# Softmax sums of a self attention: ScalarE copy and GpSimd power in place of VectorE's reciprocal, for three groups of four

## The chip, the cores and the metric

The kernel runs on one core of a Trainium2 chip. The metric is the device time of one execution in microseconds (us). The engines are TensorE (PE; PEld is its weight load), VectorE (DVE), ScalarE (ACT), GpSimd (POOL) and SyncE (SP). Each runs its own list of instructions strictly in order, and they meet only through counting semaphores.

## What is computed

A block of six residual layers over x (256 tokens of 512 features), of which the first self attention is the one that the change touches. Its reference, cut to what matters (16 heads of 32 features; `act_quant` rounds a tensor to e4m3 with one scale):

```python
qkv = jnp.einsum('bsh,hf->bsf', x, W_qkv)
q8, q_scale = act_quant(q)
k8, k_scale = act_quant(k)
scores = jnp.einsum('bhqd,bhkd->bhqk', q8, k8) * (q_scale * k_scale) / jnp.sqrt(hd)
attn = jax.nn.softmax(scores, axis=-1)
v8, v_scale = act_quant(v)
out = jnp.einsum('bhqk,bhkd->bhqd', attn, v8) * v_scale
return jnp.einsum('bsh,ho->bso', out, W_out) + b_out
```

The layers around it are a cross attention over 4096 context tokens (most of the run), a feed-forward, an attention over the context as memory, a second self attention and a mixture of experts.

## The kernel before

Everything stays on the core, and each engine's list is written out by hand: `tensor_attention`, `vector_attention`, `scalar_attention` and two GpSimd functions are called with k = 0 for the first self attention and k = 1 for the second. The 16 heads are done in four groups f = 0 to 3 of four heads (SHG = 4), 32 partitions to a head, so that one group fills 128 partitions.

For each group the scores are made once to find each query's maximum (`scores`, L1197; VectorE's `maxima`, L1436). `split_maxima` (L1444 to L1450) turns the maxima into three bf16 parts, TensorE turns these (`turn_maxima`, L1207), ScalarE copies them (`move_maxima`, L1363), and `scores_turned` (L1220, L1224) makes the scores the other way round with the maxima subtracted. ScalarE raises them, one 128x512 Exp for each head (`raise_head`, L1373, four for each group). `weigh_group(f)` then makes, on TensorE, the sums of the exponentials (L1242, into `sum_bank(f)`, counted by `as_summed`) and the weighted values (L1250, into `value_bank(f)`, counted by `as_weighed`).

`normalise(f)` on VectorE closes a group: a reciprocal of the 128x256 sums out of PSUM into the tile `inv` (L1458), and one product of value bank, scale and `inv` into the tile xT (L1461), which counts `ao_moved`. `project_out` (L1257) multiplies xT by the output weights on TensorE; each call is two matmul rows of the trace. After it VectorE adds the result to x (L1512), and the next layer norm begins, whose `rstd` GpSimd makes as a power with exponent -0.5 (L130, 128x1).

The order that matters here, on VectorE: `maxima(2)`, `split_maxima(2)`, `normalise(0)`, `maxima(3)`, `split_maxima(3)`, `normalise(1)`, two additions of the output bias (L1504), `normalise(2)`, `normalise(3)`. On TensorE, with f counting up: `scores_turned(f)`, some dummy matmuls on `ident` that keep the engine busy (`stay_awake`, L135), the scores of the next group's last head, `weigh_group(f - 1)`; then `turn_maxima` of the next group. For f = 2 the dummies stand behind a wait for `ao_moved` 1:

```python
elif f == 2 and k == 0:
    e.wait_ge(ao_moved, 1)
    stay_awake(e, W_BANK, 3)
```

`weigh_group(2)` waits for `ao_moved` 2 ahead of its values, because the value bank of groups 0 to 2 is one and the same. The last stretch is `project_out(1, 0)`, `weigh_group(3)`, and `project_out` of the feature blocks 1, 2, 3 for tokens 0 to 127 and then for tokens 128 to 255. GpSimd has no part in the four groups: `gpsimd_quantise` (L1521) makes three maxima over all partitions before them, and `gpsimd_norm` comes after them.

Of the kernel before, what the change touches and what calls it, by code (L numbers as in the profile page):

```python
# [6 lines left out]
F32 = mybir.dt.float32  # L7
# [3 lines left out]
ALU = mybir.AluOpType  # L11
# [3 lines left out]
P = 128  # L15
T, D = 256, 512
TT, DT = T // P, D // P
# [46 lines left out]
def build(nc, a, out):  # L64
    ctx = ExitStack()
    with ctx:
        def sems(names):
            return [ctx.enter_context(nc.semaphore(n)) for n in names.split()]
# [6 lines left out]
        def place(offset, *specs):  # L75
            places[0] += 1
            with ExitStack() as scope:
                if offset:
                    sb(f"gap{places[0]}", [P, offset // 4], F32, scope)
                return [sb(n, shape, dt, scope) for n, shape, dt in specs]  # L80
# [19 lines left out]
        own = Steps(vector_step)  # L100
# [43 lines left out]
        def norm_move(e, n, i, bank):  # L144
            e.wait_ge(ln_turned, TT * n + i + 1)
            e.copy(xT[:, :, i * P:(i + 1) * P], bank.rearrange("p (c t) -> p c t", c=4)).then_inc(ln_xT, 1)
# [935 lines left out]
        SHG = P // SHD  # L1082
        RING = 2 * SHG

        def att_memory(tag):
            return place(
                WORK, (f"{tag}w_qkv", [P, 3, DT, D], F32), (f"{tag}w_out", [P, DT, D], F32), (f"{tag}b_out", [P, D], F32),
                (f"{tag}b_qk", [P, 8], F32), (f"{tag}b_v", [P, D], F32), (f"{tag}xn", [P, TT, D], F32),
                (f"{tag}qkT", [P, 8, T], F32), (f"{tag}v", [P, TT, D], F32), (f"{tag}q8", [P, 4, T], BF16), (f"{tag}k8", [P, 4, T], BF16),
                (f"{tag}v8", [P, TT, D], F32), (f"{tag}eT", [P, RING, TT * T], F32), (f"{tag}inv", [P, T], F32),  # L1090
                (f"{tag}mx", [P, 2, TT, SHG], F32), (f"{tag}rest", [P, TT, SHG], F32), (f"{tag}sc", [P, 32], F32))

        att_mem = (att_memory("l0_"), att_memory("l1_"))
        w_gate, w_router = place(WORK + 82 * KB, ("w_gate", [P, DT, NE0], F32), ("w_router", [P, DT, E], F32))

# [8 lines left out]
            "mag_found mag_max quant_scaled quant_mag quant_val quant_done")  # L1104
        as_done, as_max, as_negs, as_turned, as_moved, as_doneT, as_raised, as_summed, as_weighed, ao_moved = sems(
            "as_done as_max as_negs as_turned as_moved as_doneT as_raised as_summed as_weighed ao_moved")
        att_out, att_added = sems("att_out att_added")

        W_BANK = twin[:, D:2 * D]

# [4 lines left out]
        def turned_bank(r):  # L1115
            return banks[3 + r][:] if r < 3 else twin[:, 0:D]

        def sum_bank(f):

            return W_BANK[:, T:2 * T] if f < 2 else banks[(0, 5)[f - 2]][:, 0:T]  # L1120

        def value_bank(f):
            return W_BANK[:, 0:T] if f < 3 else banks[4][:, 0:T]

        def qk_bank(k, n):

            return banks[n][:] if k == 0 or n in (0, 2) else (banks[3][:], twin[:, 0:D])[n // 2]

        def v_bank(k, i):
            return banks[4 + i][:] if k == 0 or i == 0 else W_BANK  # L1130
# [51 lines left out]
                e.dma_start(b_v[:], a["l1_bv"].partition_broadcast(P)).then_inc(att_b_in, 16)  # L1182

        def tensor_attention(e, k):
            w, w_out, _, _, _, xn, qkT, v, q8, k8, v8, eT, _, _, _, _ = att_mem[k]
            qs, ks, vs = (q8, k8, v8) if k == 0 else (qkT[:, 0:4, :], qkT[:, 4:8, :], v)
            base = SH * k

# [142 lines left out]
        def att_mags(k):  # L1331

            xn, eT = att_mem[k][5], att_mem[k][11]
            return eT[:, RING - 2:RING, :].rearrange("p a b -> p (a b)"), xn[:].rearrange("p i d -> p (i d)")

        def scalar_attention(e, k):
            _, _, _, b_qk, _, _, qkT, v, _, _, _, eT, _, _, _, sc = att_mem[k]
            tensors = (qkT[:, 0:4, :], qkT[:, 4:8, :], v[:])

            def scale_to_e4m3(n):  # L1340
                t = tensors[n]
                m = att_mags(k)[n % 2].rearrange("p (a b) -> p a b", a=t.shape[1])
                e.wait_ge(quant_scaled, n + 1)
                if n == 2:
                    e.wait_ge(quant_done, 1)
                e.activation(m, t, ACT.Copy, scale=sc[:, 22 + n:23 + n]).then_inc(quant_mag, 1)
                e.wait_ge(quant_mag, n + 1)
                e.activation(t, t, ACT.Copy, scale=sc[:, 6 + n:7 + n]).then_inc(quant_val, 1)

            def move_qk(f):  # L1350
                e.wait_ge(qk_projected, 4 * k + QK_ORDER[k].index(f) + 1)
                if k == 0:
                    t = e.copy(qkT[:, f - 1:f + 1, :].rearrange("p a t -> p (a t)"), qk_bank(k, f // 2))
                else:
                    for g in (f - 1, f):
                        t = e.activation(qkT[:, g, :], qk_bank(k, f // 2)[:, (g % 2) * T:(g % 2 + 1) * T], ACT.Identity, bias=b_qk[:, g:g + 1])
                t.then_inc(qk_moved, 1)

            def move_maxima(f):
                e.wait_ge(as_turned, 4 * k + f + 1)  # L1360
                if f >= 2:
                    e.wait_ge(as_doneT, 4 * k + f - 1)
                e.copy(negsT[:, f % 2, :], turned_bank(0)[:, 0:T]).then_inc(as_moved, 1)  # L1363

            def raise_head(f, r):
                h = SHG * f + r
                if r == 0:
                    e.wait_ge(as_doneT, 4 * k + f + 1)
                    if f >= 2:
                        e.wait_ge(as_weighed, 4 * k + f - 1)  # L1370
                if k == 0 and h == RING - 2:
                    e.wait_ge(quant_done, 3)
                e.activation(eT[:, h % RING, :], turned_bank(r), ACT.Exp,  # L1373
                             scale=sc[:, 9:10] if k == 0 else A_SCALE).then_inc(as_raised, 1)

            if k == 0:
                for i in range(TT):
                    norm_move(e, 1, i, banks[2 * i][:])
            else:
                norm_move(e, 4, 1, av_bank(1))  # L1380
                e.wait_ge(att_b_in, ATT_B[1])
            for f in QK_ORDER[k][0:2]:
                move_qk(f)
            if k == 0:
                scale_to_e4m3(0)
            for f in QK_ORDER[k][2:4]:
                move_qk(f)
            if k == 0:
                scale_to_e4m3(1)
                for i in range(TT):  # L1390
                    e.wait_ge(av_projected, i + 1)
                    e.copy(v[:, i, :], v_bank(k, i)).then_inc(av_moved, 1)
                scale_to_e4m3(2)
            for f in range(4):
                move_maxima(f)
                for r in range(SHG):
                    raise_head(f, r)

        def vector_attention(e, k):
            _, _, b_out, _, b_v, xn, qkT, v, q8, k8, v8, _, inv, mx, rest, sc = att_mem[k]  # L1400
            tensors = (qkT[:, 0:4, :], qkT[:, 4:8, :], v[:])

            def largest(n):
# [46 lines left out]
                e.tensor_tensor(parts[:, :, :, 2], rest[:], parts[:, :, :, 1], ALU.subtract).then_inc(as_negs, 1)  # L1450

            def normalise(f):
                e.wait_ge(as_summed, 4 * k + f + 1)
                if f < 2:
                    e.wait_ge(as_weighed, 4 * k + f + 1)
                if f:
                    e.wait_ge(ao_moved, 4 * k + f)
                own.done(e.reciprocal(inv[:], sum_bank(f)))  # L1458
                own.wait(e)
                e.wait_ge(as_weighed, 4 * k + f + 1)  # L1460
                e.scalar_tensor_tensor(xT[:, f, :], value_bank(f), sc[:, 5:6] if k == 0 else 1.0, inv[:],  # L1461
                                       ALU.mult, ALU.mult).then_inc(ao_moved, 1)
# [27 lines left out]
            for f in range(1, 4):  # L1490
# [7 lines left out]
                if f == 1 and k:  # L1498
                    add_v_bias(1)
            normalise(1)  # L1500
            if k == 0:
                e.wait_ge(att_b_in, ATT_B[0])
# [12 lines left out]
                norm_apply(e, n_norm, i, xn_next)  # L1515

        def gpsimd_quantise(e):
            sc = att_mem[0][-1]
            for n in range(3):
                e.wait_ge(mag_found, n + 1)  # L1520
                e.partition_all_reduce(sc[:, n:n + 1], sc[:, 10 + n:11 + n], P, bass.bass_isa.ReduceOp.max).then_inc(mag_max, 1)  # L1521

        w_up, w_down, w_exp, _, hT, xn3, g3 = place(
            WORK, ("w_up", [P, DT, D], F32), ("w_down", [P, DT, D], F32), ("w_exp", [P, DT, D], F32),
            ("gap_wout", [P, DT * D + 2 * D + 8], F32),
            ("hT", [P, DT, T], F32), ("xn3", [P, TT, D], F32), ("g3", [P, 64], F32))
# [156 lines left out]
        def av_bank(i):  # L1685
            return twin[:, i * D:(i + 1) * D]
# [787 lines left out]
```

## Time and profile before

| | |
|---|---|
| median of 3 runs | 1639.95 us (1639.75 to 1640.92) |
| the profiled execution | 1641.43 us, its span from first to last instruction 1639.6 us |
| mean granted TensorE clock | 0.999 |
| busy share of the span | PE 98%, VectorE 66%, ScalarE 42%, GpSimd 8% |
| the first self attention's four groups | from about 1191.6 to 1223.6 us of the span |

A row of a timeline gives the start in us from the span's start, how long it lasts, the engine, the line of the kernel, the operation with what it writes and reads, how many instructions were merged, and in brackets the idle time ahead of it with the engine that ended it. A row of merged instructions lasts from the first one's start to the last one's end. A row of the chain of waits gives start, length and what the run's end was waiting for at that time, "issue" being time in which the engine waited for nothing that the profile shows. Matmul ends are modelled, and durations on GpSimd are rough.

### The profile page before, as it was taken

What the parts mean: (1) busy time and instruction counts of PE and PEld (TensorE: products, weight loads), DVE (VectorE), ACT (ScalarE), POOL (GpSimd) and SP (SyncE); (2) the same over time, 40 slices, a digit from 0 to 9 for tenths busy, and PEclk for the clock granted to TensorE, in tenths of its full rate; (3) what the DMA queues carried; (4) which work ended last, traced back from release to release, by engine and by line L of the source; (5) the groups of instructions that cost most, each with busy time, mean ns of one, the idle gap of its engine ahead of it and who ended that gap; (6) DMA issues with size and microseconds to landing.
All of it is one profiled execution on the core that took longest, in us unless ns stands there. A gap on an engine that the chain in (4) does not pass through costs nothing.

```text
span 1639.6 us, 22511 instructions
## 1 busy us (share of the span) xinstructions
PE 1611.7 (98%) x8732; PEld 1250.7 (76%) x8732; DVE 1086.7 (66%) x1733; ACT 690.1 (42%) x933; POOL 131.0 (8%) x218
## 2 busy tenths in 40 slices
PE   9999999999999999999999999999999999999998
PEld 7887888888888888888888888887757746555454
DVE  4445777777778778777777779999583741743333
ACT  4334454444445454444454446555331321322221
POOL 0001000000100000010000001111100000011110
PEclk9999999999999999999999999999999999999999
DMA  7876655554565556555454454334320517479994
GB/s 237 226 227 189 161 132 154 149 151 122 170 163 142 148 142 154 119 184 142 119 138 124 128 135 123 102 92 150 121 112 18 205 52 287 197 233 427 422 423 183
DMA packets 125513, 282.93 MB, mean 173 GB/s; under 512 B 7712, under 2 KB 83680, under 8 KB 119264
## 3 DMA queue, kind: packets, MB, share of 16 engines
q1 hardware_dynamic: 103104, 200.75, 38.8%
q0 software_dynamic: 22304, 80.75, 16.5%
q8 instruction: 70, 1.15, 0.3%
q14 instruction: 35, 0.29, 0.1%
HBM read 206.99 MB, written 74.48 MB: 172 GB/s over the span
## 4 chain that ended last, share of the span: by engine, by line
PE 84%; DVE 8%; issue 3%; ACT 3%; DMA 2%; POOL 0%; SPq 0%; DVEq 0%; ACTq 0%
PE bank L478 19%; PE bank L41 19%; PE bank L448 17%; PE bank L500 6%; PE bank L2109 5%; PE bank L1728 3%; PE bank L499 3%; PE bank L2148 2%; PE bank L2134 2%; PE bank L526 1%; DVE e_parts L851 1%; PE bank L2138 1%; DVE S L830 1%; PE bank L2094 1%; DMA v_dram<-v_out 1%
## 5 line engine op out<-in xcount | busy, mean ns | idle before, releaser
L478 PE MATMUL bank<-wv_parts,cT_hi 128*128 128x512 f32 x1024 | 333.8, 390 | 1.7 <-DMA wv_parts<-wv_dram 1.6
L478 PEld LDWEIGHTS bank<-wv_parts,cT_hi 128*128 128x128 f32 x1024 | 192.3, 188 | 42.4 <-DMA wv_parts<-wv_dram 2.0
L851 DVE TENSOR_TENSOR e_parts<-S,e_parts 128x1024 fp32r<-128x1024 f32 (+1 forms) x129 | 156.8, 1215 | 85.5 <-ACT e_parts L656 83.3
L448 PE MATMUL bank<-cT_hi,wk_hi 128*128 128x512 f32 x512 | 204.7, 400 | 0.7 <-DVE cT_lo L783 0.7
L448 PE MATMUL bank<-cT_hi,wk_lo 128*128 128x512 f32 x512 | 199.8, 390 | 0.0
L448 PE MATMUL bank<-cT_lo,wk_hi 128*128 128x512 f32 x512 | 199.7, 390 | 0.0
L647 ACT ACTIVATE S<-S 128x1024 f32<-128x1024 f32 (+1 forms) x129 | 135.8, 1053 | 151.7 <-DVE S L830 151.1
L478 PE MATMUL bank<-wv_parts,cT_lo 128*128 128x512 f32 x512 | 199.3, 389 | 0.0
L843 DVE TENSOR_TENSOR esum<-esum,S 128x512 f32<-128x512 f32 x210 | 144.9, 690 | 71.7 <-ACT S L647 68.1
L656 ACT CAST e_parts<-S 128x1024 fp32r<-128x1024 f32 (+1 forms) x129 | 134.8, 1045 | 135.7 <-PE bank L500 129.5
L803 DVE TENSOR_TENSOR mx<-mx,S 128x512 f32<-128x512 f32 x222 | 152.8, 688 | 13.5 <-ACT S L641 9.6
L830 DVE TENSOR_TENSOR S<-S,mrow 128x1024 f32<-128x1024 f32 (+1 forms) x129 | 155.4, 1207 | 0.4 <-POOL mrow L1050 0.4
L500 PE MATMUL bank<-e_parts,v_back 128*128 128x512 f32 x424 | 154.2, 397 | 0.0
L41 PE MATMUL bank<-q_hi,k_hi 128*128 128x256 f32 x512 | 146.1, 285 | 4.6 <-DVE k_lo L790 4.5
L41 PE MATMUL bank<-q_lo,k_hi 128*128 128x256 f32 x512 | 144.8, 283 | 0.0
L41 PE MATMUL bank<-q_hi,k_lo 128*128 128x256 f32 x512 | 144.8, 283 | 0.0
L625 ACT CAST k_hi<-bank 128x512 fp32r<-128x512 f32 x128 | 75.3, 588 | 156.6 <-PE bank L448 156.6
L641 ACT COPY S<-bank 128x1024 f32<-128x1024 f32 x128 | 129.1, 1009 | 13.5 <-PE bank L41 8.3
L1037 POOL DMA_DIRECT2D v_back<-v_dram x110 | 59.1, 537 | 837.4 <-PE bank L500 826.9
L499 PE MATMUL bank<-e_parts,v_back 128*128 128x256 f32 x424 | 122.9, 290 | 0.2
L856 DVE TENSOR_TENSOR v_out<-bank,v_out 128x512 fp32r<-128x512 f32 x112 | 76.9, 686 | 62.9 <-ACT v_out L668 62.9
L448 PEld LDWEIGHTS bank<-cT_hi,wk_lo 128*128 128x128 f32 x512 | 96.2, 188 | 22.5 <-issue 2.2
(289 smaller groups left out, 2588.4 us busy)
## 6 DMA issues: line engine op xcount, KB each, us to landing
w<-in_w_moe SPq DMA_DIRECT2D x32, 2304.0 KB, 16.6
v_dram<-v_out SPq DMA_DIRECT2D x112, 512.0 KB, 5.0
v_back<-v_dram POOLq DMA_DIRECT2D x110, 512.0 KB
ctx_nat<-in_ctx SPq DMA_DIRECT2D x8, 1024.0 KB, 4.9
ctx_raw<-in_ctxT SPq DMA_DIRECT2D x7, 1024.0 KB, 8.5
v_dram<-v_back SPq DMA_DIRECT2D x14, 512.0 KB, 4.5
v_late<-v_dram POOLq DMA_DIRECT2D x14, 512.0 KB
wv_parts<-wv_dram POOLq DMA_DIRECT2D x6, 1024.0 KB, 8.7
```

Source lines behind the costliest of these rows:

```text
L41: last = e.matmul(dst, lhs, rhs, start=(n == 0), stop=(n == len(terms) - 1))
L448: t = e.matmul(banks[b][:], l, r, start=(c == 0 and m == 0), stop=(c == DT - 1 and m == 2))
L478: t = e.matmul(banks[b][:], l, r, start=(c == 0 and m == 0), stop=(c == DT - 1 and m == 2))
L499: e.matmul(*low, start=False, stop=False)
L500: t = e.matmul(*wide, start=False, stop=(j == NCH - 1 and i == CT - 1))
L641: e.copy(S[:, j * CT:(j + 1) * CT, :].rearrange("p a t -> p (a t)"), twin[:]).then_inc(s_stored, 1)
L647: e.activation(Sj, Sj, ACT.Exp).then_inc(raised, 1)
L656: e.copy(e_place(n)[:, 0, of_chunk(0, m), :], S[:, of_chunk(j, m), :]).then_inc(e_rounded, 1)
L803: own.done(e.tensor_tensor(mx[:], mx[:], two, ALU.max))
L830: e.tensor_tensor(Sj, Sj, mrow[:].unsqueeze(1).to_broadcast([P, CT if m is None else CT // 2, T]), ALU.subtract).then_inc(shifted, 1)
L843: e.tensor_tensor(esum[:], esum[:], two, ALU.add).then_inc(e_summed, 1)
L851: e.tensor_tensor(lo, S[:, of_chunk(j, m), :], hi.bitcast(F32), ALU.subtract).then_inc(e_split, 1)
```

## The change

For the first self attention alone (k = 0) and for groups 0, 1 and 2, VectorE's reciprocal is taken out of `normalise`. ScalarE copies the sums out of PSUM into a new tile `sums` in SBUF (`copy_sums(f)`, placed after the Exps of group f + 1), and GpSimd raises them to the power -1 into `inv` with a tensor_tensor whose second operand is a 128x1 tile of -1.0 broadcast over 256 columns. VectorE then only waits for `sums_inverted` and multiplies. Group 3, and all of the second self attention, keep the reciprocal on VectorE.

```diff
+            def copy_sums(f):
+                e.wait_ge(as_summed, f + 1)
+                if f < 2:
+                    e.wait_ge(as_weighed, f + 1)
+                if f:
+                    e.wait_ge(sums_inverted, f + 1)
+                e.copy(sums[:], sum_bank(f)).then_inc(sums_copied, 1)
+
             for f in range(4):
                 move_maxima(f)
                 for r in range(SHG):
                     raise_head(f, r)
+                if f and k == 0:
+                    copy_sums(f - 1)
...
             def normalise(f):
-                e.wait_ge(as_summed, 4 * k + f + 1)
-                if f < 2:
-                    e.wait_ge(as_weighed, 4 * k + f + 1)
-                if f:
-                    e.wait_ge(ao_moved, 4 * k + f)
-                own.done(e.reciprocal(inv[:], sum_bank(f)))
-                own.wait(e)
+                if f < 3 and k == 0:
+                    e.wait_ge(sums_inverted, f + 2)
+                else:
+                    e.wait_ge(as_summed, 4 * k + f + 1)
+                    if f < 2:
+                        e.wait_ge(as_weighed, 4 * k + f + 1)
+                    if f:
+                        e.wait_ge(ao_moved, 4 * k + f)
+                    own.done(e.reciprocal(inv[:], sum_bank(f)))
+                    own.wait(e)
                 e.wait_ge(as_weighed, 4 * k + f + 1)
                 e.scalar_tensor_tensor(xT[:, f, :], value_bank(f), sc[:, 5:6] if k == 0 else 1.0, inv[:],
                                        ALU.mult, ALU.mult).then_inc(ao_moved, 1)
...
         def gpsimd_quantise(e):
...
+            e.memset(minus[:], -1.0).then_inc(sums_inverted, 1)
+            e.wait_ge(sums_inverted, 1)
+            for f in range(3):
+                e.wait_ge(sums_copied, f + 1)
+                if f:
+                    e.wait_ge(ao_moved, f)
+                e.tensor_tensor(inv[:], sums[:], minus[:].to_broadcast([P, T]), ALU.pow).then_inc(sums_inverted, 1)
```

How the lists of instructions stand, at three places. ScalarE, over the four groups (l_eT are the exponentials, negsT the turned maxima; lines with + are new):

```order
 L1363 CAST negsT<-bank 128x256
 L1373 ACTIVATE l_eT<-bank,l_sc 128x512 x4
+L1400 COPY l_sums<-bank 128x256
 L1363 CAST negsT<-bank 128x256
 L1373 ACTIVATE l_eT<-bank,l_sc 128x512 x4
+L1400 COPY l_sums<-bank 128x256
 L1363 CAST negsT<-bank 128x256
 L1373 ACTIVATE l_eT<-bank,l_sc 128x512 x4
+L1400 COPY l_sums<-bank 128x256
```

Each copy of a group's sums stands behind the four Exps of the next group and, but for the last, ahead of the copy of the maxima of the one after. VectorE with the change, from the second group's end on (L1446 are the maxima, L1474 the product into xT, L1471 the reciprocal):

```order
L1446 TENSOR_REDUCE l_mx<-bank 128x2 x4
L1454 TENSOR_SCALAR negs<-l_mx 128x8
L1456 SCALAR_TENSOR_TENSOR l_rest<-l_mx,negs 128x8
L1458 CAST negs<-l_rest 128x8
L1460 TENSOR_TENSOR negs<-l_rest,negs 128x8
L1474 SCALAR_TENSOR_TENSOR xT<-bank,l_sc,l_inv 128x256
L1517 TENSOR_TENSOR x<-x,l_b_out 128x512 x2
L1474 SCALAR_TENSOR_TENSOR xT<-bank,l_sc,l_inv 128x256
L1471 RECIPROCAL l_inv<-bank 128x256
L1474 SCALAR_TENSOR_TENSOR xT<-bank,l_sc,l_inv 128x256
```

Three reciprocals are gone; the products stay where they were, and the fourth group's reciprocal stands behind the third group's product. GpSimd with the change (the rows of ISA without a tile load a library; L1534 are the maxima over partitions):

```order
L1162 CAST ident_bf<-ident 128x128
L1534 ISA
L1534 ISA l_sc<-l_sc 128x1 x3
L1535 MEMSET l_minus 128x1
L1541 ISA
L1541 TENSOR_TENSOR l_inv<-l_sums,l_minus 128x256 x3
L130 TENSOR_TENSOR rstd<-vareps,half 128x1 x4
```

The library load that stood right ahead of the four `rstd` now stands ahead of the three new powers; the `rstd` come behind them.

## Rows read from the trace of the kernel before

**Rows 1.** The page: span, busy time of each engine.

```profile
span 1639.6 us, 22511 instructions
PE 1611.7 (98%) x8732; PEld 1250.7 (76%) x8732; DVE 1086.7 (66%) x1733; ACT 690.1 (42%) x933; POOL 131.0 (8%) x218
```

**Rows 2.** The chain of waits, 1205.9 to 1221.2 us (start, length, what).

```profile
1205.98 1.76 DVE l_inv L1458
...
1211.74 0.27 PE bank L1207 x2
...
1218.26 2.79 PE bank L1257 x6
...
1221.14 0.70 DVE x L1512
```

**Rows 3.** VectorE's timeline, 1205.9 to 1224.3 us.

```profile
1207.77 0.49 DVE L1461 SCALAR_TENSOR_TENSOR xT<-bank,l_sc,l_inv 128x256 f32<-128x256 f32 x1
...
1213.35 0.48 DVE L1461 SCALAR_TENSOR_TENSOR xT<-bank,l_sc,l_inv 128x256 f32<-128x256 f32 x1
...
1217.47 1.76 DVE L1458 RECIPROCAL l_inv<-bank 128x256 f32<-128x256 f32 x1 [0.25 <-PE bank L1242]
1219.26 0.48 DVE L1461 SCALAR_TENSOR_TENSOR xT<-bank,l_sc,l_inv 128x256 f32<-128x256 f32 x1
1221.14 0.69 DVE L1512 TENSOR_TENSOR x<-bank,x 128x512 f32<-128x512 f32 x1 [1.40 <-PE bank L1257]
...
1222.81 0.15 DVE L119 TENSOR_SCALAR vareps<-meanvar 128x1 f32<-128x1 f32 x1
1223.69 0.55 DVE L123 TENSOR_SCALAR xn<-x,meanvar,rstd 128x512 f32<-128x512 f32 x1 [0.73 <-POOL rstd L130]
```

**Rows 4.** TensorE's timeline, 1204.6 to 1223.7 us.

```profile
1204.61 1.05 PE L1250 MATMUL bank<-l_eT,l_v 128*32 128x256 f32 x16
...
1208.31 0.94 PE L135 MATMUL bank<-ident 128*128 128x128 f32 x6 [0.72 <-DVE xT L1461]
...
1210.38 1.05 PE L1250 MATMUL bank<-l_eT,l_v 128*32 128x256 f32 x16
...
1214.30 1.05 PE L1250 MATMUL bank<-l_eT,l_v 128*32 128x256 f32 x16
...
1218.19 5.42 PE L1257 MATMUL bank<-l_w_out,xT 128*128 128x512 f32 x12
```

**Rows 5.** ScalarE's timeline, 1206.5 to 1216 us.

```profile
1206.54 0.37 ACT L1363 CAST negsT<-bank 128x256 bf16<-128x256 f32 x1 [2.50 <-PE bank L1207]
...
1212.05 0.37 ACT L1363 CAST negsT<-bank 128x256 bf16<-128x256 f32 x1 [1.98 <-PE bank L1207]
1213.53 2.42 ACT L1373 ACTIVATE l_eT<-bank,l_sc 128x512 f32<-128x512 f32 x4 [1.11 <-PE bank L1224]
```

**Rows 6.** GpSimd's timeline, 1178 to 1224 us.

```profile
1178.13 0.38 POOL L1521 PARTITION_ALL_REDUCE l_sc<-l_sc  x1 [9.64 <-DVE l_sc L1408]
...
1192.22 0.35 POOL L1521 PARTITION_ALL_REDUCE l_sc<-l_sc  x1 [6.67 <-DVE l_sc L1408]
1223.06 0.60 POOL L130 TENSOR_TENSOR rstd<-vareps,half 128x1 f32<-128x1 f32 x1 [30.48 <-DVE vareps L119]
```

**Rows 7.** One line's operations: L130 (duration in ns: minimum, median, maximum).

```profile
L130 POOL TENSOR_TENSOR rstd<-vareps,half x12: 549/570/1008, 5.7 to 1430.5; 128x1 f32<-128x1 f32 x12
```

**Rows 8.** GpSimd's groups by shape (busy us, mean ns of one).

```profile
L2017 POOL CAST gate_parts<-ids_i 128x128 fp32r<-128x128 int32 x1 | 0.9, 888 | 0.1
...
L1162 POOL CAST ident_bf<-ident 128x128 bf16<-128x128 f32 x1 | 0.3, 287 | 0.0
...
L2014 POOL CAST slot_col<-slot_col_i 128x1 f32<-128x1 int32 x1 | 0.2, 188 | 0.0
```

**Rows 9.** By stretch: PE, PEld, DVE, ACT, POOL busy; granted clock, DMA share, GB/s.

```profile
1206.00:1211.74 5.74, 4.02 (x59) 2.27 (x60) 5.49 (x12) 2.79 (x5) 0.00 (x0) 1.00 0.01 3
```

More of the change, by code:

```diff
@@ L1090, in att_memory @@
                 (f"{tag}v8", [P, TT, D], F32), (f"{tag}eT", [P, RING, TT * T], F32), (f"{tag}inv", [P, T], F32),
-                (f"{tag}mx", [P, 2, TT, SHG], F32), (f"{tag}rest", [P, TT, SHG], F32), (f"{tag}sc", [P, 32], F32))
+                (f"{tag}mx", [P, 2, TT, SHG], F32), (f"{tag}rest", [P, TT, SHG], F32), (f"{tag}sc", [P, 32], F32), (f"{tag}sums", [P, T], F32), (f"{tag}minus", [P, 1], F32))
         att_mem = (att_memory("l0_"), att_memory("l1_"))
@@ L1106, in build @@
             "as_done as_max as_negs as_turned as_moved as_doneT as_raised as_summed as_weighed ao_moved")
-        att_out, att_added = sems("att_out att_added")
+        att_out, att_added, sums_copied, sums_inverted = sems("att_out att_added sums_copied sums_inverted")
         W_BANK = twin[:, D:2 * D]
@@ L1184, in tensor_attention @@
         def tensor_attention(e, k):
-            w, w_out, _, _, _, xn, qkT, v, q8, k8, v8, eT, _, _, _, _ = att_mem[k]
+            w, w_out, _, _, _, xn, qkT, v, q8, k8, v8, eT = att_mem[k][:12]
             qs, ks, vs = (q8, k8, v8) if k == 0 else (qkT[:, 0:4, :], qkT[:, 4:8, :], v)
@@ L1336, in scalar_attention @@
         def scalar_attention(e, k):
-            _, _, _, b_qk, _, _, qkT, v, _, _, _, eT, _, _, _, sc = att_mem[k]
+            _, _, _, b_qk, _, _, qkT, v, _, _, _, eT, _, _, _, sc, sums, _ = att_mem[k]
             tensors = (qkT[:, 0:4, :], qkT[:, 4:8, :], v[:])
@@ L1397, in scalar_attention @@
                     raise_head(f, r)
+                if f and k == 0:
+                    copy_sums(f - 1)
         def vector_attention(e, k):
-            _, _, b_out, _, b_v, xn, qkT, v, q8, k8, v8, _, inv, mx, rest, sc = att_mem[k]
+            _, _, b_out, _, b_v, xn, qkT, v, q8, k8, v8, _, inv, mx, rest, sc, _, _ = att_mem[k]
             tensors = (qkT[:, 0:4, :], qkT[:, 4:8, :], v[:])
@@ L1517, in gpsimd_quantise @@
         def gpsimd_quantise(e):
-            sc = att_mem[0][-1]
+            inv, _, _, sc, sums, minus = att_mem[0][12:]
             for n in range(3):
```

## Prediction

> **What bounds the kernel now.** The page says that TensorE is busy for 98% of the span and VectorE for 66% [rows 1]; such averages say little of a stretch of 20 us, so I read the stretch itself, first in the chain of waits. What the run's end waits for there is VectorE until 1211.6 us, with the first group's reciprocal in the middle of it (1205.98, 1.76 us), and from 1211.74 us TensorE, without a break until VectorE adds the projected tile at 1221.14 [rows 2]. So the first of the reciprocals stands on the path, and the later ones run beside TensorE.
>
> VectorE's timeline gives the moments at which the products into xT start and end: group 0 at 1207.77, group 1 at 1213.35, and group 3 from 1219.26 to 1219.74 [rows 3]. TensorE's timeline tells who waits: its dummy matmuls start at 1208.31, after 0.72 us of idling for group 0's product; the values of group 2, which need group 1's product, start at 1214.30; the last projections start at 1218.19 [rows 4]. The end is tight: the third projection of tokens 0 to 127 needs group 3's product, which ends at 1219.74, and its two predecessors (four of the twelve rows that share 5.42 us) end near 1220.0. A product that comes later is soon paid for one for one.
>
> **The change part by part.** Let X be the time that GpSimd needs for one 128x256 power. Everything else can be read.
>
> *Copies.* Three 128x256 copies out of PSUM by ScalarE, at 0.37 us each, the price of its 128x256 cast out of PSUM [rows 5]. The first comes when the values of group 0 are done, 1204.61 + 1.05 = 1205.66, plus 0.04 from TensorE to ScalarE (1211.74 + 0.27 to 1212.05 [rows 2, 5]): 1205.70 to 1206.07, in the 2.50 us that ScalarE idles ahead of 1206.54. The second can run from 1211.47 to 1211.84, in the idle time ahead of 1212.05. These two cost nothing by themselves. The third stands behind the last four Exps, which end at 1213.53 + 2.42 = 1215.95, so it runs from 1215.99 to 1216.36; nothing of this layer is queued behind it on ScalarE.
>
> *Handovers.* From VectorE to GpSimd it takes 0.10 us (1222.81 + 0.15 to 1223.06), and back 0.03 us (1223.66 to 1223.69) [rows 3, 6]. I use these for ScalarE to GpSimd as well.
>
> *Library load.* The load that stood ahead of `rstd` now stands ahead of the first power, with no wait of its own. The last maximum over partitions ends at 1192.57 and the first copy at 1206.07, 13.5 us later. Ahead of the maxima the same kind of load fitted into an idle time of 9.64 us [rows 6]. I cost it at nothing; were it exposed, it would add what remains of it to group 0. The memset of one column beside it lies in the same gap.
>
> *Group 0.* The power starts at 1206.17, and the product at 1206.20 + X in place of 1207.77: a shift of X - 1.57, which I call D. Behind that wait on VectorE stand the maxima and the split of group 3, and behind these TensorE's turn of the maxima at 1211.74. D goes to the path whole if positive, and also, up to about 0.7 us, if negative.
>
> *Group 1.* The values end at 1210.38 + 1.05 = 1211.43 + D; copy and handovers add 0.04 + 0.37 + 0.10, so the power starts at 1211.94 + D and the product ends at 1212.45 + D + X. TensorE's values of group 2 want that at 1214.30 + D, so up to X = 1.8 nothing waits here.
>
> *Group 2.* This power needs the third copy and, since it overwrites `inv`, group 1's product. The first gives 1216.46 + D, the second 1212.55 + D + X; they cross at X = 3.91. Its product takes 0.03 + 0.48, and only then does VectorE reach group 3's reciprocal (0.04 + 1.76) and product (0.03 + 0.48), where today the reciprocal starts at 1217.47, as soon as its sums are there.
>
> *Sum.* Below the crossing, group 3's product ends at 1216.46 + D + X + 0.51 + 0.04 + 1.76 + 0.51 = 1219.28 + D + X. Against 1219.74 that is D + X - 0.46 = **2X - 2.03**. Above it, it ends at 1212.55 + D + 2X + 2.82 = 1215.37 + D + 2X, which is **3X - 5.94** late. In words: below the crossing one power and the tail are on the path; above it, all three stand in a row. The three reciprocals of 1.76 us that leave VectorE are in these sums already.
>
> *The size of X.* The trace of before has the power only on one column: 549 ns at least, 570 at the median [rows 7]. From below: 0.55 plus 255 columns at the price of a plain cast, (287 - 188) / 127 = 0.78 ns each, is 0.75 us. From above: a one-column cast takes 188 ns, so the arithmetic of the power is 549 - 188 = 361 ns for one column, and if each of 256 columns pays that in turn, X = 0.19 + 92.4 = 92.6 us [rows 7, 8]. Between ends so far apart I take the geometric middle, 8.3 us, moved a little towards the upper end because that one comes from the row of the same operation: **X = 10 us**, which says that the loop overlaps some nine columns. Then D = 8.4 and the sum is 3 x 10 - 5.94 = 24.1 us.
>
> *The clock.* With X = 10 TensorE would idle for more than 8 us at a time. The trace shows nothing like it: even in the stretch around group 0, with TensorE busy 4.02 of 5.74 us, the granted clock is 1.00, the level of 2.4 GHz [rows 9]. A fall to 1.2 GHz would matter only where TensorE sets the pace, in the eight projection rows behind the last wait: 8 x 5.42 / 12 = 3.6 us more at most, none at least. I add the half, 1.8 us. The Trainium skill (TensorE: Matmul & The Clock Gate, section "What's actually happening") says that an idle TensorE falls to half its rate and has to be busy again to regain it; by that it would be the upper end, and no run here shows it yet.
>
> Together 24.1 + 1.8 = 25.9 us. On the profiled execution's own 1641.43 us that is 1667.3; this execution lies 1.48 us above the median of the runs, 1639.95, so for the median I predict **1666 us**.
>
> **The rivals.** *GpSimd is quick enough (no change).* If the columns stream, X lies between the lower end, 0.75, and the price of the slowest plain row, (888 - 188) / 127 = 5.5 ns a column, which gives 0.55 + 1.41 = 1.96 us [rows 8]. The sum is then -0.5 to +1.9 us, with 1.3 us in the middle +0.6: 1640.5 us. It decides for X below 2.65, where 2X - 2.03 reaches 3.3 us. For it: one column costs only 0.36 us more than a cast, which may be depth rather than rate. Against it: streaming at a few ns a column means that a hundred columns are in work at once. The Trainium skill (GPSIMD Engine Reference, section "Elementwise — side-by-side cycle accounting") gives 2.6 cycles an element for an addition with two inputs; an estimate from that page is 256 x 2.6 / 1.2 GHz = 0.55 us on top of the one-column power, X = 1.1 and a change of +0.2 us. It speaks for this rival, but of additions, and no run here shows it. Faster by over 0.2% (3.3 us, about what a measurement of this kernel can tell from no change) cannot come out of the sum: at the lower end of X it is -0.5.
>
> *No overlap at all (much slower).* X = 92.6, the sum 3 x 92.6 - 5.94 = 271.9, with the clock 1913 us. For it: the one-column row taken at its word. Against it: the loop over columns would have to start each only when the one before is finished.
>
> *The powers are not where the wait is.* If the library is loaded only when the first power comes up, its unknown remainder is added to D once. Against it: `rstd` at 1223.06 started 0.10 us after its input, long after its load [rows 6]. I give it no chance of its own.
>
> **How the numbers follow.** Forecast (X from 2.65 to 32): 0.62, with 1643 to 1733 as its own range; X = 32 gives 90.1 + 3.6 us. GpSimd quick: 0.23. Little or no overlap (X over 32): 0.15. The range reaches down to the quick case's lower end, 1639, since without it 0.38 would be left out, and up to 1733; about 0.16 is outside. Slower: 0.62 + 0.15 = 0.77; faster 0.01; the rest, 0.22, within 0.2%.
>
> **What would show it.** In the profile of the changed kernel the three rows of the power give X at once, and the formula then has to give the time: three rows of about 10 us, VectorE idle ahead of each product for the GpSimd tile, TensorE idle ahead of the dummy matmuls by some 9 us and ahead of group 2's values by some 8, the third power starting right after group 1's product. With X near 1 the chain would show TensorE as before, with VectorE's last reciprocal starting near 1218. A time that doesn't fit 2X - 2.03 or 3X - 5.94 for the X that is seen would mean that I have a wait wrong; a granted clock under 1.00 after the idle times would size the last term.

## The result and the profile after

The changed kernel takes 1761.35 us (median of 4 runs, 1760.84 to 1761.66) against 1640.28 us before (4 runs): a ratio of 1.0736, 95% interval 1.0721 to 1.0751. It is slower by 121 us. The prediction said 1666, with a range of 1639 to 1733: the sign was right, the time lies outside the range. The profiled execution has a span of 1759.9 us in place of 1639.6.

The page of the changed kernel, its span, its busy times and one of its costliest groups:

```profile
span 1759.9 us, 22518 instructions
...
PE 1617.5 (92%) x8732; PEld 1252.7 (71%) x8732; DVE 1082.3 (61%) x1730; ACT 690.5 (39%) x936; POOL 254.5 (14%) x222
...
L1541 POOL TENSOR_TENSOR l_inv<-l_sums,l_minus 128x256 f32<-128x256 f32 x3 | 123.7, 41243 | 20.7 <-ACT l_sums L1400 20.0
```

Every engine did about the work that it did before [rows 1]; GpSimd alone has 123.5 us more, and its three powers of 41.2 us take 123.7. Where they lie is told by the chain of waits (start, length, what the end of the run was waiting for):

```profile
1205.99 41.19 POOL l_inv L1541
...
1247.21 0.50 DVE xT L1474
...
1253.45 41.13 POOL l_inv L1541
...
1295.23 41.44 POOL l_inv L1541
...
1337.28 1.77 DVE l_inv L1471
...
1339.61 1.74 PE bank L1257 x2
```

In [rows 2] the same place held one reciprocal of 1.76 us and then TensorE. Now all three powers stand in the chain one behind the other. VectorE's timeline has the places of [rows 3] (start, duration, operation, and in brackets the idle time ahead and what ended it):

```profile
1247.21 0.48 DVE L1474 SCALAR_TENSOR_TENSOR xT<-bank,l_sc,l_inv 128x256 f32<-128x256 f32 x1 [41.44 <-POOL l_inv L1541]
...
1294.60 0.48 DVE L1474 SCALAR_TENSOR_TENSOR xT<-bank,l_sc,l_inv 128x256 f32<-128x256 f32 x1 [42.99 <-POOL l_inv L1541]
...
1336.69 0.48 DVE L1474 SCALAR_TENSOR_TENSOR xT<-bank,l_sc,l_inv 128x256 f32<-128x256 f32 x1 [39.99 <-POOL l_inv L1541]
1337.28 1.76 DVE L1471 RECIPROCAL l_inv<-bank 128x256 f32<-128x256 f32 x1
1339.07 0.48 DVE L1474 SCALAR_TENSOR_TENSOR xT<-bank,l_sc,l_inv 128x256 f32<-128x256 f32 x1
```

VectorE idles 124.4 us for the three tiles. The copies by ScalarE took 0.37 us each, as worked out. TensorE's rows answer to [rows 4]:

```profile
1247.75 1.65 PE L135 MATMUL bank<-ident 128*128 128x128 f32 x6 [40.47 <-DVE xT L1474]
...
1251.57 1.31 PE L1250 MATMUL bank<-l_eT,l_v 128*32 128x256 f32 x16
...
1295.14 1.93 PE L1250 MATMUL bank<-l_eT,l_v 128*32 128x256 f32 x16 [39.58 <-DVE xT L1474]
...
1337.23 2.08 PE L1257 MATMUL bank<-l_w_out,xT 128*128 128x512 f32 x2 [34.82 <-DVE xT L1474]
```

It waits at the places of the prediction's walk, and its first work after a wait is slow: the six dummy rows take 1.65 us in place of 0.94, group 1's values 1.31 in place of 1.05. By stretch (length, busy time of PE, PEld, DVE, ACT and POOL, granted clock, DMA share, GB/s):

```profile
1214.00:1247.00 33.00, 0.00 (x0) 0.00 (x0) 0.00 (x0) 0.00 (x0) 33.00 (x1) 0.50 0.00 0
1247.00:1250.00 3.00, 2.25 (x12) 1.62 (x16) 2.31 (x5) 0.00 (x0) 0.18 (x1) 0.50 0.00 0
1250.00:1254.00 4.00, 4.00 (x40) 1.59 (x42) 1.40 (x5) 0.65 (x2) 0.55 (x1) 0.74 0.00 0
1254.00:1258.00 4.00, 1.57 (x33) 0.69 (x32) 0.00 (x0) 2.42 (x4) 4.00 (x1) 1.00 0.00 0
...
1336.00:1340.00 4.00, 2.46 (x3) 0.89 (x4) 2.73 (x3) 0.00 (x0) 0.66 (x1) 0.50 0.00 0
```

While all engines but GpSimd stand still, the clock granted to TensorE goes to 0.50, the level of 1.2 GHz. TensorE starts again at 1247.75, and the clock is back at 1.00 in the stretch from 1254 us on.

### The profile page after: what moved, and what is told of

The parts are those of the page before. It is cut to its first block, busy times and chain, and to the rows that moved or that the text cites. A ratio compares the mean times of both kernels' runs of the same rounds, so it can differ in the third digit from the quotient of the medians.

```text
span 1759.9 us, 22518 instructions
## 1 busy us (share of the span) xinstructions
PE 1617.5 (92%) x8732; PEld 1252.7 (71%) x8732; DVE 1082.3 (61%) x1730; ACT 690.5 (39%) x936; POOL 254.5 (14%) x222
## 4 chain that ended last, share of the span: by engine, by line
PE 78%; POOL 7%; DVE 7%; ACT 3%; issue 3%; DMA 2%; SPq 0%; DVEq 0%; ACTq 0%; POOLq 0%
PE bank L478 18%; PE bank L41 17%; PE bank L448 16%; POOL l_inv L1541 7%; PE bank L500 6%; PE bank L2129 5%; PE bank L1748 3%; PE bank L499 3%; PE bank L2168 2%; PE bank L2154 2%; PE bank L526 1%; PE bank L2158 1%; DVE e_parts L851 1%; DVE S L830 1%; PE bank L2114 1%
## 5 line engine op out<-in xcount | busy, mean ns | idle before, releaser
L1541 POOL TENSOR_TENSOR l_inv<-l_sums,l_minus 128x256 f32<-128x256 f32 x3 | 123.7, 41243 | 20.7 <-ACT l_sums L1400 20.0
```

The source lines that it names most:

```text
L1541: e.tensor_tensor(inv[:], sums[:], minus[:].to_broadcast([P, T]), ALU.pow).then_inc(sums_inverted, 1)
```

## How the traces are compared

Outside the attention the traces of two executions differ by up to a microsecond or two, so I measure inside the stage: from the start of group 2's maxima on VectorE, the last work that nothing in the change can touch, to the end of group 3's product. The maxima before and in the changed kernel:

```profile
1202.66 2.48 DVE L1436 TENSOR_REDUCE l_mx<-bank 128x2 f32<-128x512 f32 x4
```

```profile
1202.35 2.48 DVE L1446 TENSOR_REDUCE l_mx<-bank 128x2 f32<-128x512 f32 x4
```

Before, that is 1202.66 to 1219.74 [rows 3], 17.08 us. In the changed kernel it is 1202.35 to 1339.55, 137.20 us, so the stage is 120.12 us longer. Of the 120.3 us by which the span grew, that is nearly all.

## The experiments

The theory after the result, A: each column of a power is paid in turn, at 41.2 us / 256 = 0.161 us, and the three powers stand on the path exactly as the prediction's formula has it. Its rivals: a large fixed price or a disturbance by other engines makes 41 us; the time is in the waits around the power; the price hangs on the values.

### e1_probe: the power by itself

In the kernel before, into GpSimd's idle time behind the maxima over partitions:

```diff
+            for n in (1, 2, 4, 8, 16, 32, 64):
+                e.tensor_tensor(tried[:, at:at + n], base[:, 0:n], power[:, 0:1].to_broadcast([P, n]), ALU.pow)
+                at += n
+            e.tensor_tensor(tried[:, at:at + 128], base[:, 0:128], power[:, 0:1].to_broadcast([P, 128]), ALU.mult)
```

and ahead of the second self attention seven powers of 32 columns: a base of 1.5 with the exponents -1, -0.5, 1, 2 and 0, and the bases 100 and 1 with -1.

> The kernel before with powers of 1, 2, 4, 8, 16, 32 and 64 columns and one product of 128 columns added on GpSimd in the idle time behind the three maxima, and seven powers of 32 columns with other exponents and bases in its idle time ahead of the second self attention. Theory A (each column is paid in turn, none overlaps): 41.2 us / 256 = 0.161 us a column, so 64 columns 10.3 to 10.7 us, 32 columns 5.2 to 5.6, and a line through 1 column at 0.55 us; the product of 128 columns under 1 us. Theory B (a large fixed share, such as code fetched at the start, or other engines disturbing GpSimd during the attention): 64 columns far above 10.7 us or the steps not in proportion. If the price hangs on the values (rival to A: a slow path for exponent -1), the seven powers differ by over 10%. The total time stays within 0.2% of before, as all of it lies in idle time.

GpSimd's groups by shape (busy us, mean ns of one, idle time ahead):

```profile
L1538 POOL TENSOR_TENSOR l_tried<-l_base,l_power 128x64 f32<-128x64 f32 x1 | 10.5, 10512 | 0.0
L1538 POOL TENSOR_TENSOR l_tried<-l_base,l_power 128x32 f32<-128x32 f32 x1 | 5.4, 5403 | 0.0
L1538 POOL TENSOR_TENSOR l_tried<-l_base,l_power 128x16 f32<-128x16 f32 x1 | 2.9, 2883 | 0.0
...
L1538 POOL TENSOR_TENSOR l_tried<-l_base,l_power 128x2 f32<-128x2 f32 x1 | 0.7, 695 | 0.0
L1538 POOL TENSOR_TENSOR l_tried<-l_base,l_power 128x1 f32<-128x1 f32 x1 | 0.6, 588 | 10.9 <-issue 10.9
L1540 POOL TENSOR_TENSOR l_tried<-l_base,l_power 128x128 f32<-128x128 f32 x1 | 0.4, 390 | 0.0
```

From 32 to 64 columns the power takes 5.11 us more, 160 ns a column; from 64 to the 256 of the changed kernel (41.18) it is 30.67 / 192 = 160 ns again. The fixed share is 10.51 - 64 x 0.160 = 0.3 us. Every further column costs about the same, here beside the other engines at work and in the changed kernel with all others idle: theory A holds for the price. Whether neighbouring columns overlap within these 160 ns, durations alone can't tell. The seven variants, with another moment of the program around them:

```profile
L1168 POOL TENSOR_TENSOR l_tried<-l_base,l_power x7: 5408/5409/5482, 1391.0 to 1423.4; 128x32 f32<-128x32 f32 x7
```

They differ by 1.4%, so among the five exponents and three bases tried it doesn't matter which, not even an exponent of 1 or 0. A product of 128 columns takes 0.39 us, so its price per column is about a hundredth of the power's.

One expectation failed: the total was not unchanged but 1647.94 us (one run). The first power started only 10.9 us after the memsets, waiting for nothing that the profile shows; I read this as the library load, whose instruction stands there; the seven powers further on, which have no such instruction ahead of them, started right behind their memsets. The powers then ended at 1225.9, and the next layer norm's `rstd`, behind them on GpSimd, came at 1226.26, 3.6 us after it could have started. The other 3.9 us of the 7.5 are not accounted for, and one run can't tell them from spread: the runs of before around it lie between 1638.82 and 1647.50 us. I take the load up below.

### e2_cols64, e3_cols16, e4_product: the same plan with other prices

```diff
-e.tensor_tensor(inv[:], sums[:], minus[:].to_broadcast([P, T]), ALU.pow)
+e.tensor_tensor(inv[:, 0:64], sums[:, 0:64], minus[:].to_broadcast([P, 64]), ALU.pow)   # e2_cols64
+e.tensor_tensor(inv[:, 0:16], sums[:, 0:16], minus[:].to_broadcast([P, 16]), ALU.pow)   # e3_cols16
+e.tensor_tensor(inv[:], sums[:], minus[:].to_broadcast([P, T]), ALU.mult)               # e4_product
```

In e2_cols64 and e3_cols16 a memset fills `inv` with 1.0 beforehand.

> The changed kernel with each power on the first 64 of 256 columns only; the other 192 columns of the groups 0 to 2 are left uninverted (the factor stays 1). Theory A: X = 10.3 to 10.7 us, and the prediction's formula 3X - 5.94 gives +25.0 to +26.2 us, with the clock term up to 3.6 more: 1665 to 1670 us, which is the forecast as it stood. Rival (the time is not in the power but in the waits around it): well over 1670 us, near 1761.

> The changed kernel with each power on the first 16 of 256 columns only; the other columns of the groups 0 to 2 are left uninverted. Theory A: X = 2.6 to 3.0 us, below the crossing at 3.91, so 2X - 2.03 = +3.2 to +4.0 us, 1643.5 to 1644.5 us. Rival (the three handovers cost more than the 0.5 us each that were worked out): above 1646 us.

> The changed kernel with a product in place of the power on GpSimd, 256 columns as there; the inversion of the sums of groups 0 to 2 is left out. It prices the plan of the change without the power. By the formula with X = 0.75 to 1.3 us: -0.5 to +0.6 us, no change within 0.2%. Rival (the path through ScalarE and GpSimd costs by itself): slower by over 0.2%. Second rival (freeing VectorE of three reciprocals of 1.76 us is worth most of 5.3 us): faster by over 0.2%.

These runs were compared with 23 runs of before around them (median 1640.44). Medians: e2_cols64 1671.08 us, ratio 1.0176 (1.0154 to 1.0199); e3_cols16 1647.76 us, 1.0036 (1.0026 to 1.0046); e4_product 1640.53 us, 0.9992 (0.9979 to 1.0004). So the time follows the price of the power, and the plan around it costs nothing that these runs can tell, with an operation of 0.61 us in the power's place. Equally, three reciprocals less on VectorE are worth nothing that can be told here; inside the stage it is 0.7 us.

The first power of e2_cols64, and of e3_cols16, and the durations of e4_product's products:

```profile
1205.57 10.58 POOL L1542 TENSOR_TENSOR l_inv<-l_sums,l_minus 128x64 f32<-128x64 f32 x1 [13.46 <-ACT l_sums L1400]
```

```profile
1205.83 2.95 POOL L1542 TENSOR_TENSOR l_inv<-l_sums,l_minus 128x16 f32<-128x16 f32 x1 [13.45 <-ACT l_sums L1400]
```

```profile
L1541 POOL TENSOR_TENSOR l_inv<-l_sums,l_minus x3: 612/612/613, 1204.7 to 1213.9; 128x256 f32<-128x256 f32 x3
```

e2_cols64 is the forecast's own case, X near 10 us. It came out at 1671 us, 5 us above the forecast and 1 us above the range expected here; its rival, near 1761, is out. Of the 5 us, 1.9 are the powers (the formula gives +26.0 for their durations in place of 24.1), and 2.1 are what the stage lost beyond the formula. e3_cols16 was expected at 1643.5 to 1644.5 and is 3 us above that. Its rival was that the handovers cost more than worked out; but from the copies' ends to the powers' starts it took 0.07 to 0.16 us, against 0.10 worked out. TensorE's rows and the stretches of e3_cols16 tell where the time went:

```profile
1209.35 0.94 PE L135 MATMUL bank<-ident 128*128 128x128 f32 x6 [2.24 <-DVE xT L1474]
...
1211.78 1.95 PE L1250 MATMUL bank<-l_eT,l_v 128*32 128x256 f32 x16
```

```profile
1206.50:1209.40 2.90, 0.66 (x17) 0.36 (x17) 0.58 (x2) 2.23 (x4) 2.28 (x1) 1.00 0.02 6
1209.40:1211.00 1.60, 1.60 (x17) 1.10 (x21) 1.60 (x3) 0.19 (x1) 0.00 (x0) 1.00 0.00 0
1211.00:1213.00 2.00, 2.00 (x24) 1.02 (x20) 1.43 (x6) 0.00 (x0) 0.00 (x0) 0.52 0.00 0
1213.00:1215.00 2.00, 2.00 (x12) 0.64 (x4) 0.00 (x0) 0.65 (x2) 0.73 (x1) 0.63 0.00 0
```

TensorE had idled 2.24 us ahead of its dummies, was fully busy again from 1209.35 on, and yet its granted clock fell to 0.52 from 1211 to 1213: the values of group 1 took 1.95 us there in place of 1.05 [rows 4], the sums ahead of them 1.49 in place of 1.07, so 1.3 us of the 1.4 that the stage lost beyond the formula are here. The single runs fit this: three of the twelve took 1644.6 to 1645.4 us at a mean granted clock of 0.998 or 0.999, the nine others 1647.1 to 1648.4 us at 0.995 to 0.997. The rest of the 7.3 us by which the median grew, about 2 us, lies outside the stage and was not followed.

### e5_group0, e6_group2: one power at a time

```diff
-                if f < 3 and k == 0:
+                if f < 1 and k == 0:      # e5_group0 (e6_group2: f == 2)
```

and the copy and the power for that group alone.

> The changed kernel with the copy and the power for group 0 alone; groups 1 to 3 keep VectorE's reciprocal. Theory A (each power stands on the path by itself, and the three add): X = 41.2 us, so X - 1.57 = +39.6 us, and about 2 us more because TensorE restarts at the lower granted clock: 1681 to 1683 us. Rival (a first power alone is partly hidden, and it is the queue of three that costs): under 1670 us.

> The changed kernel with the copy and the power for group 2 alone; groups 0, 1 and 3 keep VectorE's reciprocal. Theory A: the power starts near 1216.5 us in place of a reciprocal at 1214.95, and group 3's reciprocal and product stand behind it: X - 0.46 = +40.8 us, with 0.5 to 3 us more for the clock in the projections behind it: 1681 to 1684 us. Rival (TensorE's own work in the last stretch hides part of it): under 1675 us.

Measured: 1683.80 us (2 runs, ratio 1.0264, 1.0243 to 1.0284) and 1682.62 us (2 runs, 1.0256, 1.0236 to 1.0277). One power in either place costs nearly its whole length, less the 1.57 and 0.46 us of the formula. The rivals, 1670 and 1675 us, are out. What follows the power differs; group 3's product in e5_group0 and in e6_group2:

```profile
1260.37 0.48 DVE L1474 SCALAR_TENSOR_TENSOR xT<-bank,l_sc,l_inv 128x256 f32<-128x256 f32 x1
```

```profile
1258.11 0.48 DVE L1472 SCALAR_TENSOR_TENSOR xT<-bank,l_sc,l_inv 128x256 f32<-128x256 f32 x1
```

From the maxima of group 2 (1202.10 and 1200.81) the stage is 41.67 us longer in e5_group0 and 40.70 us in e6_group2; the formula's terms are 41.18 - 1.57 = 39.61 and 41.18 - 0.46 = 40.72. The second is exact. The first is 2.06 us short, and what lies between the power and group 3's product in that run, but not in e6_group2, is TensorE's work after a long idle time. Behind the stage it is the other way round: in e6_group2 VectorE's second addition of a projected tile comes 5.99 us after group 3's product, against 4.41 before: 1.6 us lost, within the 0.5 to 3 that were expected for the clock there.

### e7_awake, e8_awake_short: TensorE kept busy in the waits

```diff
                 elif f == 2 and k == 0:
+                    e.wait_ge(as_raised, SHG * 3)
+                    stay_awake(e, banks[3], 160)     # e7_awake: 340
                     e.wait_ge(ao_moved, 1)
```

and in the same way 160 (340) dummies ahead of group 2's values and 145 (320) ahead of the second feature block's projection.

> The changed kernel with 340, 340 and 320 more dummy matmuls of 128 columns on TensorE in the three long waits, so that it isn't idle in them; nothing else differs. If the granted clock is what remains between the formula (3 x 41.2 - 5.94 = 117.8 us) and the measured 120.3 us of the span, the clock stays at 1.00 in the windows behind the waits, TensorE's dummies to group 1's values take 3.2 us again in place of 5.2, and the time falls by 2 to 4 us, to 1757 to 1759 us. Rival (the remainder is not the clock): the time stays at 1761 us within 1 us.

> As e7_awake with 160, 160 and 145 dummies, since one dummy took 0.224 to 0.231 us there (two instructions) and not 0.11: 160 x 0.231 = 37 us, which ends inside each wait. If the granted clock is what remains between the formula (117.8 us) and the 120.3 us measured, the windows behind the waits show 1.00, the stretch from group 0's product to group 1's copy takes about 2 us less than in the changed kernel, and the time falls by 2 to 4 us, to 1757 to 1759 us. Rival (the remainder is not the clock): 1761 us within 1 us.

e7_awake is a miss of mine: a dummy is two instructions, the 340 took 78 us, and the run took 1869.09 us (ratio 1.1396). It told the right count for e8_awake_short: 1759.44 us, ratio 1.0726 (1.0709 to 1.0744), 1.9 us under the changed kernel, though the intervals of the two overlap and the median lies just outside both the expected 1757 to 1759 us and the rival's 1760 to 1762. The times leave it open; the stage in the trace decides. Group 0's product, the second power and the stretches of e8_awake_short:

```profile
1247.02 0.48 DVE L1481 SCALAR_TENSOR_TENSOR xT<-bank,l_sc,l_inv 128x256 f32<-128x256 f32 x1 [41.43 <-POOL l_inv L1548]
```

```profile
1251.23 41.12 POOL L1548 TENSOR_TENSOR l_inv<-l_sums,l_minus 128x256 f32<-128x256 f32 x1 [4.25 <-ACT l_sums L1407]
```

```profile
1245.00:1248.00 3.00, 2.69 (x25) 2.50 (x24) 0.98 (x2) 0.00 (x0) 1.98 (x1) 1.00 0.00 0
1248.00:1250.00 2.00, 2.00 (x31) 1.21 (x33) 1.89 (x5) 0.00 (x0) 0.00 (x0) 1.00 0.00 0
...
1302.00:1334.00 32.00, 28.36 (x254) 28.16 (x253) 0.00 (x0) 0.00 (x0) 32.00 (x1) 1.00 0.00 1
...
1336.00:1340.00 4.00, 3.70 (x5) 1.18 (x4) 1.73 (x3) 0.00 (x0) 0.00 (x0) 0.50 0.00 0
```

Behind the first wait the clock is at 1.00, and from group 0's product to the start of the second power it takes 1251.23 - 1247.02 = 4.21 us, where the changed kernel took 1253.45 - 1247.21 = 6.24: the 2.0 us are the clock. From group 2's maxima to group 3's product the stage is now 118.10 us longer than before, against the formula's 117.79. The last dummies ended 4.7 us too early, and the clock fell again ahead of the last projections, so the loss there was not undone. The span of this execution, 1759.8 us, is no shorter than the changed kernel's: what the stage won, it lost outside the stage, 0.6 us of it in the last projections; the rest was not followed.

### e9_log_exp: the inversion on ScalarE

```diff
-                e.copy(sums[:], sum_bank(f)).then_inc(sums_copied, 1)
+                e.activation(sums[:], sum_bank(f), ACT.Ln).then_inc(sums_copied, 1)
+                e.wait_ge(sums_copied, f + 1)
+                e.activation(inv[:], sums[:], ACT.Exp, scale=-1.0).then_inc(sums_inverted, 1)
```

> Another place for the inversion: ScalarE makes exp(-ln(sum)) for groups 0 to 2, straight out of the sum bank, and GpSimd has no part. Each needs two table loads of 1.28 us (as the two in the trace of before) and two activations of 0.37 us, 3.3 us in all. By the same walk along the path: group 0's product 1.3 us late, the copy of group 2's maxima 2.5 us late, that of group 3's maxima 4.6 us late, group 3's product 6 to 7 us late: +6 to +8 us, 1646 to 1648 us. Rival (ScalarE's idle time hides it): within 0.2% of before.

1651.35 us, ratio 1.0070 (1.0053 to 1.0087), slower than expected by another 3 to 5 us. ScalarE's timeline for group 0:

```profile
1205.68 1.28 ACT L1400 ACT_TABLE_LOAD   x1 [1.72 <-PE bank L1250]
1206.98 0.38 ACT L1400 ACTIVATE l_sums<-bank 128x256 f32<-128x256 f32 x1
1207.38 1.28 ACT L1402 ACT_TABLE_LOAD   x1
1208.67 0.42 ACT L1402 ACTIVATE l_inv<-l_sums 128x256 f32<-128x256 f32 x1
```

The 3.3 us came as worked out; inside the stage the loss is 8.2 us. TensorE idled 2.99 us behind the late copy of the maxima and then ran at 0.50 from 1211 to 1213, which the expectation did not have; a second idle time of 2.70 us was followed by no such fall:

```profile
1209.40 0.29 PE L1220 MATMUL bank<-l_q,l_k 32*128 32x256 bf16 x4 [2.99 <-ACT negsT L1363]
...
1218.47 0.29 PE L1220 MATMUL bank<-l_q,l_k 32*128 32x256 bf16 x4 [2.70 <-ACT negsT L1363]
```

```profile
1211.00:1213.00 2.00, 2.00 (x16) 0.79 (x19) 1.32 (x4) 1.50 (x3) 0.00 (x0) 0.50 0.00 0
...
1218.00:1222.00 4.00, 3.53 (x54) 1.62 (x58) 1.68 (x3) 3.25 (x7) 0.00 (x0) 1.00 0.00 0
```

The rest of the difference to the runs' 11.4 us (an interval from 8.7 to 14.3) lies outside the stage or in the spread of the runs, and was not followed. So this is no way out either.

No version beat the kernel before. e4_product shows about what this plan could win at best by taking the three reciprocals off VectorE: 0.7 us in the stage.

## Why the prediction was wrong

By its own steps, with the lengthening of the stage as measured and as its formula gives it from the durations of the powers or products in each run:

| run | one operation, us | formula, us | measured, us |
|---|---|---|---|
| e4_product | 0.61 | 2X - 2.03 = -0.8 | -0.7 |
| e3_cols16 | 2.95 | 2X - 2.03 = +3.9 | +5.3 |
| e2_cols64 | 10.58, 10.53, 10.84 | sum - 5.94 = +26.0 | +28.1 |
| changed kernel | 41.18, 41.12, 41.43 | sum - 5.94 = +117.8 | +120.1 |
| e8_awake_short | 41.18, 41.12, 41.43 | sum - 5.94 = +117.8 | +118.1 |

**The mechanism: right.** The waits, their places, the crossing from one power on the path to three, and the cost of copies and handovers hold from 0.6 to 41 us. One wait was left out: `sums` is a single tile, so the third copy also has to wait for the second power (it ran at 1294.66 us, not behind the last Exps). It cost nothing, because the third power waits for group 1's product, which ends 0.05 us behind that copy. The rival "GpSimd is quick enough" would have come true with an operation that streams, as e4_product shows.

**The size of X: wrong, and this is the step that failed.** "From above: a one-column cast takes 188 ns, so the arithmetic of the power is 549 - 188 = 361 ns for one column", and from below 0.75 us; the prediction then took X = 10 us, "which says that the loop overlaps some nine columns". Measured: 160 ns for each further column, 41.2 us. Of the 361 ns some 200 do not come back with every column (durations can't tell whether they are a fixed share or hidden behind a neighbour), so the upper end was 2.2 times too high; the point taken was 4 times too low. The bounds did hold the value, but the geometric middle between 0.75 and 92.6 us is no reading of the trace: one row of one column cannot part the fixed share from the price per column. The rival "no overlap at all" was right that each column costs a large part of what the first one does, but at 1913 us it was priced too high. The range then ended at X = 32 by my choice of 0.15 beyond it, where nothing in the rows spoke for 32.

The Trainium skill (GPSIMD Engine Reference, section "Elementwise — side-by-side cycle accounting") gives 2.6 cycles an element for an addition with two inputs; at the page's 1.2 GHz that is, as an estimate, 2.2 ns a column. The products of e1_probe and e4_product come near it, (612 - 390) / 128 = 1.7 ns; of a power the page says nothing, and 160 ns is some 90 times the product's price.

**The clock: right in kind.** Half of 3.6 us was added for the last projections. The changed kernel lost 2.0 us behind the first wait, where I had charged nothing, and less behind the last: from group 3's product to VectorE's addition it is 1341.45 - 1339.55 = 1.90 us against 1.40 before [rows 3]. At the X that the term was made for, in e2_cols64, VectorE's second addition of a projected tile came 5.86 us after group 3's product, against 4.41 before, so 1.45 us were lost there, near the 1.8. What the term left out is the loss behind the first wait.

**The library load: nothing, as costed, but by luck.** The bound of 9.64 us was that of another library's load. This one took 10.9 us in e1_probe; as long a load, begun behind the memset at 1192.3 us of the changed kernel, would end less than 3 us ahead of the first power.

## What to carry to other kernels

A duration at one size gives no price at another: where an operation stands in the trace at one column only, measure two sizes before its engine is given 256 columns of it, and until then keep the whole span between the bounds in the range. Work moved to an idle engine is only free if it is done before the next wait; here three operations of 41 us stood where 1.76 us had been, on an engine that was 8% busy. Check first what a free operation in that place would bring: with a product of 0.61 us the whole plan won 0.7 us in its stage, which twelve runs could not tell from nothing; so no price of the power down to that one could have made it worthwhile.

## What was not expected of the hardware

- A power on GpSimd costs 160 ns a column of 128 partitions (5.41 us for 32, 41.2 us for 256) whichever of the five exponents and three bases was tried, a product 1.7 ns.
- What I read as the library load for GpSimd's power took 10.9 us where nothing hid it. The configuration instruction itself shows as 83 ns, and the wait as "issue"; in e1_probe:

```profile
1203.36 22.57 POOL L1538 TENSOR_TENSOR l_tried<-l_base,l_power 128x1 f32<-128x1 f32 x7 [10.93 <-issue]
```

The Trainium skill (GPSIMD Engine Reference, section "Instruction dispatch") puts the load that the first call after such an instruction pays at about 6 us; the wait measured here is nearly twice that.

- TensorE's clock fell to 1.2 GHz behind idle times of 2.24 us (e3_cols16) and 2.99 us (e9_log_exp), and in e3_cols16 it fell only when TensorE had been at work again for 1.6 us. It cost that stage some 1.3 us. In the trace of before, idle times up to 0.72 us in this stage left it at 1.00 [rows 4, 9]. The length of an idle time alone doesn't tell: a second one of 2.70 us in e9_log_exp, ended at 1218.47 us, left the clock at 1.00 until 1231.
